# Routed attention, second pass: the row sums inverted on ScalarE by logarithm and exponential, VectorE's product one group later

## The chip, the cores and the metric

The kernel runs on one core of one Trainium2 chip. A time is microseconds (us) on the device from start to end of one execution of the whole program; the median of several runs counts. The engines named below are TensorE (PE; its weight loads are PEld), VectorE (DVE), ScalarE (ACT), GpSimd (POOL) and SyncE (SP), which issues most transfers.

## The reference, cut to what matters

A two-layer tower over 8 sequences of 512 rows with 192 features. The last layer's first half is the attention touched here: 12 heads of 16 features, softmax over 512 keys, then a projection and the residual add. Its second half sends each row to two of eight experts.

```python
x = x + _attention(_layer_norm(x, ln1_g, ln1_b), qkv_w, qkv_b, proj_w, proj_b)
    # attn = softmax(q @ k.T * 16 ** -0.5);  o = (attn @ v) merged over heads @ proj_w + proj_b
xn = _layer_norm(x, ln2_g, ln2_b).reshape(B * N, C)
    # top 2 of xn @ gate_w choose the experts of each row
return x + _moe_mlp(xn, gate_w, w1, b1, w2, b2).reshape(B, N, C)
```

The kernel doesn't divide the attention weights. It multiplies the exponentials with values that carry 16 columns of ones beside the 16 features of each head; so the read-out of a head has 16 rows of output and 16 rows that all hold the sum of the exponentials. The division comes after that, on 128 x 512 numbers for a group of four heads.

## The kernel before

The function `routed_attention` has two blocks. The first makes q, k and v and the row maxima of all batches; its last ScalarE instruction (L2272) is an exponential of one column, which brings in the table for the exponentials. The second block is the second pass, and the change is there. It is written out by hand, one program for each engine, unrolled over the eight batches (sequences) b. The engines are ordered among themselves by semaphores alone; a `Signal` counts in units per batch, and `x.wait(engine, b, k)` waits until k units of batch b are done. An engine works its own list strictly in order.

Heads come in three groups g of four (NG = 3), keys in four chunks c of 128 (T = 4). A tile n is one pair of group and chunk, n = 4 g + c, 0 to 11; it has two score tiles e = 2 n and e = 2 n + 1, each 128 keys x 2 heads x 512 queries.

- TensorE, for each n: the scores of tile n + 1 (L2500, four matmuls into PSUM; a score buffer is used again every third e, so scores e wait until exponential e - 3 is done); then the read-out of tile n (L2566), which needs the exponentials of n, summed over the four chunks of a group in one bank. Between these stands the rest of the previous batch: behind n = 2 and 3 the two halves of its projection (L2513), ahead of the second half the ranks of the batch before that (L2535, L2537), which wait for the first half's residual add; behind n = 8 and 9 the turning of its normed rows for the gate (L2519), the first of them waiting for the norm (`xa`) and for the copy of the present batch's group 1, whose bank it takes; behind n = 11 the gate's logits (L2527).
- ScalarE, for each e: the exponential (L2618, 128 x 1024). Behind e = 19 and 21 it copies the turned rows of the previous batch (L2611).
- VectorE, for each batch: sets up the residual rows, adds the previous batch's projection (L2646), with the ranks read between the halves and the places behind them, row statistics and norm constants (L2653 to L2658). Then for each group: ahead of g = 1 the norm (L2665), which waits for GpSimd's power (L2779); ahead of g = 2 the logits (L2678, L2682); then it waits for the group's read-out, copies it from PSUM to `OS` (L2730), makes a small read of it (L2732), shuffles the sums' rows over the outputs' rows into `OT` (L2734), takes their reciprocal (L2735) and multiplies it with `OS` in `OT` (L2736). The last product of a batch releases its projection (`ot`). Behind the groups it searches the two best logits of each row of the previous batch (L2688 to L2696).
- GpSimd: four indirect sends of rows, the power, four more sends, two products that scale the turned rows. The first sends of a batch wait for VectorE's places.
- SP loads the q and k of the batch after next when the scores of the present one are done.

Of the kernel before, what the change touches and what calls it, by code (L numbers as in the profile page):

```python
# [12 lines left out]
ALU = mybir.AluOpType  # L13
ACT = mybir.ActivationFunctionType
# [4 lines left out]
B, S, D = 8, 512, 192  # L19
# [5 lines left out]
NH, HD = 12, 16  # L25
NG, HG = 3, 4
# [1987 lines left out]
def routed_attention(nc, m, io):  # L2014
# [25 lines left out]
    spare = g2(P, [1])  # L2040
# [12 lines left out]
    sem = lambda name: SEMS.new(nc, name)  # L2053
# [3 lines left out]
    to, oq, pr, hh = Signal(nc, "qa_out_scaled", 1, 1), Signal(nc, "qa_out_rounded", 1, 1), \  # L2057
        Signal(nc, "qa_projected", 1, 2), Signal(nc, "qa_stream_updated", 1, 2)
    S1 = lambda n, per=1, credit=1: Signal(nc, f"ra_{n}", per, credit)
# [30 lines left out]
    def turned_parts(u, bank):  # L2090
        return (BT[:, 2 * u:2 * u + 2, :].rearrange("p b s -> p (b s)"), ps[0:3 * NH, bank, :].bitcast(BF16))
# [13 lines left out]
    with nc.Block(no_gpsimd_drain=True) as block:  # L2105
# [94 lines left out]
        @block.scalar  # L2200
        def _(act):
            for s in (xc, qc, vd, p1, to):
                s.start(act)
            for k in range(2):
                act.sem_inc(s_wr[k], 1)

            def scaled(b):
                oq.wait(act, b, 0)
                act.activation(TMP, OF[:, b, :, :], ACT.Identity, bias=magic, scale=inv3).then_inc(to.sem, 1)

            def deviation(some, n):

                act.wait_ge(s_v4, n)
                out = m.wk[2][:, some, :]
                if n % 2:
                    act.activation(out, m.var[:, some, :], ACT.Sqrt, bias=m.eps, scale=1.0 / D).then_inc(s_s4, 1)
                else:
                    act.activation(out, out, ACT.Sqrt, bias=m.eps).then_inc(s_s4, 1)

            def turned(b):  # L2220
                xt.wait(act, b, 1)
                for c in range(NC):
                    ins = act.activation(XT[b % 2][0:DC, c, :], ps[0:DC, banks(b, 0) + c, :], ACT.Identity,
                                         bias=gb[:, 1, c:c + 1], scale=gb[:, 0, c:c + 1])
                ins.then_inc(xc.sem, 1)

            for b in range(4):
                scaled(b)
            deviation(slice(0, 2), 1)
            scaled(4)  # L2230
            deviation(slice(0, 2), 2)
            scaled(5)
            act.wait_ge(s_w, 16 * (5 + HG))
            turned(0)
            scaled(6)
            for b in range(B):
                for k in range(2):
                    act.wait_ge(s_wr[k], 16 * 3 * b + 1)
                for s in range(2 * NC):
                    k, c = s // NC, s % NC  # L2240
                    if b == 0 and s == NC:
                        scaled(7)
                    if c == 0:
                        p2.wait(act, b, k - 1)
                    qp.wait(act, b, s + 1)
                    bank = ps[0:DC, banks(b, k) + c, :]
                    act.activation(QK[k][:, c, :], bank, ACT.Copy)
                    act.activation(PT[k][0][:, c, :], bank, ACT.Copy).then_inc(qc.sem, 1)
                for k in range(2):
                    rest.wait(act, b, k + 1)  # L2250
                    act.activation(PT[k][1], QK[k], ACT.Copy).then_inc(p1.sem, 1)
                if b + 1 < B:
                    turned(b + 1)
                if b == 0:
                    deviation(slice(2, B), 3)
                qp.wait(act, b, 5)
                Vb = V[:, b, :].rearrange("p (t h k d) -> p t h k d", t=T, h=NH, k=2)
                for u in range(2):
                    ins = act.activation(Vb[:, 2 * u:2 * u + 2, :, 0, :], ps[:, banks(b, 0) + u, 0:2 * D].rearrange(
                        "p (t h d) -> p t h d", t=2, h=NH), ACT.Copy)  # L2260
                act.activation(Vb[:, :, :, 1, :], m.one.to_broadcast([P, T * NH * HD]).rearrange(
                    "p (t h d) -> p t h d", t=T, h=NH), ACT.Copy)
                if b == 0:
                    deviation(slice(2, B), 4)
                    to.wait(act, B - 1, 1)
                ins = act.activation(ST_[b % 2][1][KR:KR + 3, 3 * (b // 2):3 * (b // 2) + 3, :], m.one[KR:KR + 3].to_broadcast(
                    [3, 3 * S]).rearrange("p (h s) -> p h s", h=3), ACT.Copy)
                ins.then_inc(vd.sem, 1)
            for u in range(AHEAD // 2):
                act.wait_ge(s_bt, u + 1)  # L2270
                act.activation(*turned_parts(u, 4 + u), ACT.Copy).then_inc(s_bc, 1)
            act.activation(spare, m.one, ACT.Exp)  # L2272

        @block.gpsimd
        def _(pool):
# [173 lines left out]
    OT, OS = g4(P, [NG, S]), g4(P, [NG, S])  # L2449
    VT = V.rearrange("p b (t h n) -> p b t h n", t=T, h=NH)  # L2450
    NS = NG * T
    st, ex, av = S1("scores_turned", 2 * NS, 2 * NS + 1), S1("exp", 2 * NS, 3), S1("read_out", NS, NS + 1)
    os_, sh, ot, pr, xx = S1("out_copied", NG), S1("sums_placed", NG), S1("out_normalised"), \
        S1("projected", 2), S1("x_stored", 2)
    s_l3 = sem("ra_out_chain")
    SG = lambda n, per=1: Signal(nc, f"ra_gate_{n}", per, 0)
    gv, gr, xa, gt, gc, lp, lc, mk, rk, po = SG("var"), SG("rstd"), SG("rows_normed"), SG("rows_turned", 2), \
        SG("rows_turned_copied", 2), SG("logits"), SG("logits_copied"), SG("masks"), SG("ranks"), SG("places")
# [10 lines left out]
    with nc.Block(no_gpsimd_drain=True) as block:  # L2469
# [135 lines left out]
        @block.scalar  # L2605
        def _(act):
            ex.start(act)
            def turned_copy(p, c, bank):
                gt.wait(act, p, c + 1)
                lp.wait(act, p, 0)  # L2610
                act.activation(XT2[:, c, :], ps[0:DC, bank, :], ACT.Identity, bias=gb2[:, 1, c:c + 1],  # L2611
                               scale=gb2[:, 0, c:c + 1]).then_inc(gc.sem, 1)

            for b in range(B):
                for e in range(2 * NS):
                    st.wait(act, b, e + 1)
                    av.wait(act, b, e // 2 - 1)
                    act.activation(PF[e // 2 % 2][:, 2 * (e % 2):2 * (e % 2) + 2, :],  # L2618
                                   ps[:, 2 * (e % 3):2 * (e % 3) + 2, :], ACT.Exp, scale=HD ** -0.5
                                   ).then_inc(ex.sem, 1)  # L2620
                    if b and e in (19, 21):
                        turned_copy(b - 1, e // 2 - 9, 7 - b % 2)
            turned_copy(B - 1, 0, 0)
            turned_copy(B - 1, 1, 2)
            act.wait_ge(s_sc[1], 16 * T * (B - 1))
            act.wait_ge(s_gb, 2 * B)
            act.activation(XA[B % 2][:, :, HEAD:RW], XA[1 - B % 2][:, :, HEAD:RW], ACT.Copy).then_inc(s_gb, 1)
            act.wait_ge(s_d, 1)
            act.activation(d, d, ACT.Exp).then_inc(s_e, 1)

        @block.vector
        def _(v):
# [4 lines left out]
            chain, gate = Link(v, s_l3), Link(v, s_gl)  # L2637
# [67 lines left out]
            def places(p):  # L2705
# [6 lines left out]
                    v.wait_ge(s_sc[1], 16 * T * (p - 1))  # L2712
                v.tensor_copy(POS[p % 2], IF).then_inc(po.sem, 1)

            for b in range(B):
                j, rows = b % 2, X[b % 2]
                for t in range(T):
                    chain(v.tensor_scalar(rows[:, t, :], m.H[:, b, t, :], m.mean[:, b, t:t + 1], m.rstd[:, b, t:t + 1],
                                          ALU.subtract, ALU.mult))
                chain(v.tensor_tensor(rows, rows, bp[:, None, :].to_broadcast([P, T, D]), ALU.add))  # L2720
                if b:
                    add_projection(b - 1)
                    constants(b - 1)
                for g in range(NG):
                    if b and g == 1:
                        norm(b - 1)
                    if b and g == 2:
                        logits(b - 1, 7 - j)
                    av.wait(v, b, T * (g + 1))
                    v.tensor_copy(OS[:, g, :], ps[:, 6 + (j + g) % 2, :]).then_inc(os_.sem, 1)  # L2730
                    os_.wait(v, b, g + 1)
                    v.tensor_scalar(spare, OS[:, g, 0:1], 1.0, None, ALU.mult)  # L2732

                    chain(v.stream_shuffle(OT[:, g, :], OS[:, g, :], mask=[HD + n % HD for n in range(32)]))  # L2734
                    chain(v.reciprocal(OT[:, g, :], OT[:, g, :]))  # L2735
                    ins = v.tensor_tensor(OT[:, g, :], OT[:, g, :], OS[:, g, :], ALU.mult)  # L2736
                ins.then_inc(ot.sem, 1)
                if b:
                    best_two(b - 1)

            read_ranks(B - 2, 5)
            places(B - 2)
# [337 lines left out]
```

## Time and profile before

| | |
|---|---|
| median of 3 runs | 2379.43 us (2377.87 to 2382.93) |
| profiled execution | span 2403.1 us from its first to its last instruction; the page gives no other time of it |
| busy share of the span | PE 78%, PEld 42%, VectorE 62%, ScalarE 45%, GpSimd 16% |
| second pass | from 1709 to about 2009 us of the span; exponentials from 1709.0 to 1971.3 us |
| in the pass | 192 exponentials, 185.1 us; 24 reciprocals, 80.5 us |

The page gives shares over the whole span, and its chain of waits covers only the last 30 us of the program, which lie in a later stage; what the pass is worth is seen from the pass alone: its groups of instructions, its busy time batch by batch, and the order of single instructions. Times in those views count from the span's start. A number in brackets behind an instruction is the time for which its engine stood idle before it, and what ended that.

### The profile page before, as it was taken

Reading aid. Unit: us, or ns where it says so; the run is one execution under the profiler, and the core shown is the slowest. Engines: PE = TensorE matmul, PEld = TensorE weight load, DVE = VectorE, ACT = ScalarE, POOL = GpSimd, SP = SyncE. Lnnn points to the kernel's source line nnn. Section 1 sums busy time; section 2 is a strip of 40 time slices with the busy share of each in tenths; the row PEclk is TensorE's granted clock in tenths of the full one; section 3 lists DMA queues with packets and bytes.
Section 4 is the critical chain, followed back from the end, with each engine's and each line's share of the span. In section 5 each row is a group of like instructions: output and inputs, shape, how many; then the busy total and the mean of one; then the engine's idle time right before and its main releaser. Section 6 shows DMA issues by size and latency. Waiting matters only on the chain. (4 is left out here: it accounts for less than half of the span.)

```text
span 2403.1 us, 30974 instructions
## 1 busy us (share of the span) xinstructions
PE 1879.3 (78%) x9780; PEld 1007.5 (42%) x9804; DVE 1495.5 (62%) x2518; ACT 1074.7 (45%) x1896; POOL 395.9 (16%) x595
## 2 busy tenths in 40 slices
PE   3868788858876453777668877998899984999994
PEld 2745655535333320000022234442133333888883
DVE  4558449966010687999878876999788883111114
ACT  1100222214110476999979964342477661222220
POOL 5000000000112010222100003331033343222221
PEclk8989999968887575555589978997799996999997
DMA  3011110005797004443011008777666703566664
GB/s 85 1 39 31 48 31 27 20 10 229 309 411 314 20 0 127 127 127 123 18 32 40 26 16 119 130 132 107 83 88 95 97 28 135 195 201 203 202 203 184
DMA packets 147792, 264.98 MB, mean 110 GB/s; under 512 B 28864, under 2 KB 115985, under 8 KB 142678
## 3 DMA queue, kind: packets, MB, share of 16 engines
q1 hardware_dynamic: 135750, 242.10, 38.0%
q0 software_dynamic: 10768, 18.19, 2.3%
q10 hardware_dynamic: 1152, 3.15, 0.3%
q8 instruction: 67, 1.10, 0.2%
q14 instruction: 55, 0.45, 0.1%
HBM read 221.85 MB, written 57.71 MB: 116 GB/s over the span
## 5 line engine op out<-in xcount | busy, mean ns | idle before, releaser
L1743 PE MATMUL ps<-arena 128*128 x376 | 194.9, 621 | 108.2 <-ACT ps L1785 60.1
L1785 ACT ACTIVATE ps<-ps,arena 128x512 f32<-128x512 f32 x384 | 256.7, 1121 | 6.3 <-POOL arena L1769 6.3
L1753 DVE TENSOR_REDUCE arena<-ps 128x1024 f32 x192 | 232.8, 1225 | 24.5 <-PE ps L1743 12.2
L1785 ACT ACTIVATION_READ_ACCUMULATOR ps<-ps,arena 128x1 f32 x384 | 234.7, 668 | 0.0
L2159 DVE TENSOR_REDUCE arena<-ps 128x1024 f32 x192 | 221.3, 1219 | 12.4 <-PE ps L2405 9.8
L2618 ACT ACTIVATE arena<-ps 128x1024 f32<-128x1024 f32 x192 | 185.1, 1020 | 97.6 <-PE ps L2500 96.4
L2962 DVE TENSOR_TENSOR arena<-ps,arena 128x384 f32<-128x384 f32 x39 | 21.8, 558 | 286.4 <-PE ps L2918 286.4
L2942 ACT ACTIVATE arena<-ps,arena 128x256 f32<-128x256 f32 x234 | 89.5, 481 | 235.9 <-PE ps L2907 230.0
L2405 PE MATMUL ps<-arena 96*128 96x512 bf16 x500 | 162.7, 430 | 26.4 <-DVE arena L2159 12.2
L1950 ACT ACTIVATE arena<-ps 128x1024 f32<-128x1024 f32 x192 | 178.7, 1048 | 7.8 <-DVE arena L1970 4.6
L529 PE MATMUL ps<-arena 96*128 96x456 f32 (+1 forms) x512 | 170.3, 482 | 8.8 <-DMA arena<-la_xt 5.2
L2918 PE MATMUL ps<-arena 128*128 128x192 f32 x936 | 162.5, 330 | 0.7 <-DVE arena L2962 0.7
L2918 PEld LDWEIGHTS ps<-arena 128*128 128x128 f32 x936 | 151.0, 190 | 13.6 <-issue 13.6
L1970 DVE TENSOR_SCALAR arena<-arena 128x1024 bf16<-128x1024 f32 x192 | 128.6, 691 | 28.9 <-ACT arena L1950 15.0
L1743 PEld LDWEIGHTS ps<-arena 128*128 128x128 bf16 x384 | 25.8, 111 | 276.8 <-ACT ps L1785 197.4
L529 PEld LDWEIGHTS ps<-arena 96*128 96x128 f32 x512 | 96.0, 196 | 71.8 <-issue 55.4
L1903 PE MATMUL ps<-arena 128*128 (+1 forms) x368 | 113.6, 389 | 15.7 <-DMA arena<-arena 13.3
L2877 POOL DMA_INDIRECT routed_out<-arena x78 | 74.8, 958 | 281.5 <-DVE arena L2962 269.6
L2903 PE MATMUL ps<-arena 128*128 128x256 f32 x468 | 110.0, 386 | 0.5 <-ACT arena L2942 0.5
L1225 DVE COPY arena<-ps 128x768 f32<-128x768 f32 x16 | 15.3, 958 | 152.1 <-PE ps L1276 152.1
L2566 PE MATMUL ps<-arena 128*32 128x512 f32 x768 | 105.2, 620 | 3.9 <-ACT arena L2618 2.1
L2500 PE MATMUL ps<-arena 99*128 99x512 bf16 x384 | 104.1, 395 | 2.4 <-ACTq L137 2.4
(394 smaller groups left out, 3264.8 us busy)
## 6 DMA issues: line engine op xcount, KB each, us to landing
arena<-in_sm_w_dram SPq DMA_DIRECT2D x128, 576.0 KB, 15.5
arena<-in_re_w_dram SPq DMA_DIRECT2D x39, 1252.0 KB, 5.9
arena<-ra_parts SPq DMA_DIRECT2D x192, 192.0 KB, 9.1
routed_in<-routed_in SPq DMA_DIRECT2D x8, 3332.0 KB, 14.2
ra_parts<-arena SPq DMA_DIRECT2D x48, 192.0 KB, 2.4
arena<-routed_in SPq DMA_DIRECT2D x39, 196.0 KB, 5.4
arena<-la_xt SPq DMA_DIRECT2D x16, 384.0 KB, 3.4
arena<-arena SPq DMA_DIRECT2D x64, 96.0 KB, 2.2
```

Source lines behind the costliest of these rows:

```text
L529: ins = pe.matmul(ps[:, 2 * (t % 2) + bank, to:to + w], XTs[j][:, c, t * P:(t + 1) * P], Wx[:, kind, c, at:at + w], start=(c == 0), stop=( ...
L1743: ins = pe.matmul(ps[:, 2 * (n % 4) + t % 2, :], QM[j][:, h, t * P:(t + 1) * P], KI[:, b, h // HG, :], start=True, stop=True)
L1753: v.tensor_reduce(MXq[:, b, 2 * u:2 * u + 2, at_head(h)], ps[:, 2 * (n % 4):2 * (n % 4) + 2, :], AX.X, ALU.max).then_inc(s_lk, 1)
L1785: ins = act.activation(bank, bank, ACT.Exp, bias=nb[n % 4][:, t % 2:t % 2 + 1], scale=c_reg, accum_out=RS[:, b, t, at_head(h):at_head(h) + 1])
L1903: ins = pe.matmul(ps[:, 2 * (n % 3) + q, :], QM[j][:, h, c * P:(c + 1) * P], QI[:, bass.ds(b, 1), g, :].rearrange("p o s -> p (o s)"), sta ...
L1950: act.activation(PF[n % 3], ps[:, 2 * (n % 3):2 * (n % 3) + 2, :].rearrange("p a s -> p (a s)"), ACT.Exp, scale=c_reg).then_inc(pe_.sem, 1)
L1970: v.tensor_scalar(PB[n % 3], PF[n % 3], MAGIC, MAGIC, ALU.add, ALU.subtract).then_inc(rd.sem, 1)
L2159: v.tensor_reduce(MX[:, bass.ds(b, 1), 2 * (n % 2):2 * (n % 2) + 2, n // 2].rearrange("p o t -> p (o t)"), ps[:, 2 * (n % 2):2 * (n % 2) + ...
L2405: ins = pe.matmul(ps[:, t, :], ST_[j][0][0:KR, h, t * P:(t + 1) * P], ST_[j][1][0:KR, h, :], start=True, stop=True)
L2618: act.activation(PF[e // 2 % 2][:, 2 * (e % 2):2 * (e % 2) + 2, :], ps[:, 2 * (e % 3):2 * (e % 3) + 2, :], ACT.Exp, scale=HD ** -0.5).then ...
L2903: pe.matmul(unit(k), wr[:, k * P:(k + 1) * P], XT[j][:, 0, :], start=True, stop=False)
L2918: ins = pe.matmul(ps[:, 7, h * D:(h + 1) * D], HT[j][:, k, h * P:(h + 1) * P], wr[:, at:at + D], start=(k == 0), stop=(k == KH - 1))
```

## The change

ScalarE inverts the row sums in place of VectorE. Of each group, VectorE still copies the read-out, and shuffles the sums into `OT`; the shuffle now signals `sh`. ScalarE waits for that, takes the natural logarithm of `OT` in place, waits for itself, and takes the exponential of the negative of it; that signals `iv`. VectorE's product waits for `iv`; it stands one group later: the product of group 0 behind the copy of group 1, that of group 1 behind the copy of group 2 and ahead of its shuffle, and that of group 2 behind the search for the two best. On ScalarE's list the inversion of group 0 stands ahead of e = 12, that of group 1 ahead of e = 20, and that of group 2 ahead of e = 2 of the next batch (for the last batch behind all exponentials). The one-column exponential in the first block becomes a load of the table set that has both functions.

```diff
-            act.activation(spare, m.one, ACT.Exp)
+            act.preload_act_table_set("natural_log_exp_and_others")
...
-    os_, sh, ot, pr, xx = S1("out_copied", NG), S1("sums_placed", NG), S1("out_normalised"), \
+    os_, sh, ot, pr, xx = S1("out_copied", NG), S1("sums_placed", NG, 0), S1("out_normalised"), \
         S1("projected", 2), S1("x_stored", 2)
-    s_l3 = sem("ra_out_chain")
+    s_l3, s_lg = sem("ra_out_chain"), sem("ra_sums_logarithm")
+    iv = S1("sums_inverted", NG, 0)
...
+            def invert(b, g):
+                sh.wait(act, b, g + 1)
+                act.activation(OT[:, g, :], OT[:, g, :], ACT.Ln).then_inc(s_lg, 1)
+                act.wait_ge(s_lg, NG * b + g + 1)
+                act.activation(OT[:, g, :], OT[:, g, :], ACT.Exp, scale=-1.0).then_inc(iv.sem, 1)
+
             for b in range(B):
                 for e in range(2 * NS):
+                    if b and e == 2:
+                        invert(b - 1, NG - 1)
+                    if e in (12, 20):
+                        invert(b, e // 8 - 1)
                     st.wait(act, b, e + 1)
...
+            invert(B - 1, NG - 1)
             turned_copy(B - 1, 0, 0)
...
+            def normalise(b, g):
+                iv.wait(v, b, g + 1)
+                ins = v.tensor_tensor(OT[:, g, :], OT[:, g, :], OS[:, g, :], ALU.mult)
+                if g == NG - 1:
+                    ins.then_inc(ot.sem, 1)
...
                     v.tensor_copy(OS[:, g, :], ps[:, 6 + (j + g) % 2, :]).then_inc(os_.sem, 1)
+                    if g:
+                        normalise(b, g - 1)
                     os_.wait(v, b, g + 1)
                     v.tensor_scalar(spare, OS[:, g, 0:1], 1.0, None, ALU.mult)
 
-                    chain(v.stream_shuffle(OT[:, g, :], OS[:, g, :], mask=[HD + n % HD for n in range(32)]))
-                    chain(v.reciprocal(OT[:, g, :], OT[:, g, :]))
-                    ins = v.tensor_tensor(OT[:, g, :], OT[:, g, :], OS[:, g, :], ALU.mult)
-                ins.then_inc(ot.sem, 1)
+                    v.stream_shuffle(OT[:, g, :], OS[:, g, :], mask=[HD + n % HD for n in range(32)]).then_inc(sh.sem, 1)
                 if b:
                     best_two(b - 1)
+                normalise(b, NG - 1)
```

## Rows read from the trace of the kernel before

**Rows 1.** Groups, 1709 to 1985 us: line, engine, shapes, count | busy us, mean ns | idle before.

```profile
L2618 ACT ACTIVATE arena<-ps 128x1024 f32<-128x1024 f32 x192 | 185.1, 1020 | 97.6 <-PE ps L2500 96.4
...
L2735 DVE RECIPROCAL arena<-arena 128x512 f32<-128x512 f32 x24 | 80.5, 3353 | 0.8
```

**Rows 2.** Busy time by stretch: length, PE, PEld, DVE, ACT, POOL, granted clock, DMA, GB/s.

```profile
1802.00:1836.00 34.00, 31.01 (x200) 12.40 (x200) 29.75 (x63) 24.45 (x26) 13.07 (x13) 1.00 0.72 98
...
1870.00:1906.00 36.00, 33.77 (x199) 12.65 (x199) 29.70 (x63) 24.45 (x26) 13.07 (x13) 0.91 0.65 88
```

**Rows 3.** Waits, 1709 to 1985 us: who, for whom, total us, times, longest.

```profile
PE ps L2519 <- DVE arena L2730: 10.8, 7, 1.8
```

**Rows 4.** Timeline of ScalarE: start, length, instruction, count, idle before and releaser.

```profile
1708.99 1.94 ACT L2618 ACTIVATE arena<-ps 128x1024 f32<-128x1024 f32 x2 [42.46 <-PE ps L2500]
...
1716.19 27.54 ACT L2618 ACTIVATE arena<-ps 128x1024 f32<-128x1024 f32 x28 [1.75 <-PE ps L2500]
...
1797.36 3.77 ACT L2618 ACTIVATE arena<-ps 128x1024 f32<-128x1024 f32 x4
1802.79 5.87 ACT L2618 ACTIVATE arena<-ps 128x1024 f32<-128x1024 f32 x6 [1.65 <-PE ps L2500]
...
1815.75 1.94 ACT L2618 ACTIVATE arena<-ps 128x1024 f32<-128x1024 f32 x2 [2.96 <-PE ps L2500]
1818.09 7.83 ACT L2618 ACTIVATE arena<-ps 128x1024 f32<-128x1024 f32 x8 [0.40 <-PE ps L2500]
```

**Rows 5.** Timeline of TensorE, 1800 to 1837 us.

```profile
1800.35 1.95 PE L2527 MATMUL ps<-arena 96*128 96x8 f32 x16
...
1808.16 2.22 PE L2513 MATMUL ps<-arena 128*128 128x192 f32 x12
...
1812.94 0.19 PE L2535 MATMUL ps<-arena 128*128 128x40 bf16 x1 [0.70 <-DVE arena L2646]
...
1815.12 1.03 PE L2500 MATMUL ps<-arena 99*128 99x512 bf16 x4
1816.45 1.06 PE L2566 MATMUL ps<-arena 128*32 128x512 f32 x8 [0.31 <-DVE arena L2646]
...
1827.00 0.61 PE L2519 MATMUL ps<-arena 128*96 128x128 f32 x4 [1.63 <-DVE arena L2730]
...
1834.25 1.95 PE L2527 MATMUL ps<-arena 96*128 96x8 f32 x16
```

**Rows 6.** Groups of ScalarE over the whole span, shapes kept apart.

```profile
L859 ACT ACTIVATE arena<-arena 128x528 f32<-128x528 f32 x32 | 20.6, 642 | 116.7 <-DVE arena L806 116.7
...
L2272 ACT ACT_TABLE_LOAD x1 | 1.3, 1283 | 0.0
```

**Rows 7.** Timeline of VectorE, 1800 to 1837 us.

```profile
1802.45 0.68 DVE L2730 COPY arena<-ps 128x512 f32<-128x512 f32 x1
...
1803.24 0.75 DVE L2734 STREAM_SHUFFLE arena<-arena 128x512 f32<-128x512 f32 x1
...
1807.41 0.69 DVE L2736 TENSOR_TENSOR arena<-arena 128x512 f32<-128x512 f32 x1
...
1809.57 0.19 DVE L2696 TENSOR_TENSOR arena<-arena 128x32 bf16<-128x32 f32 x1
...
1815.32 0.19 DVE L2702 TENSOR_TENSOR arena<-ps,arena 128x32 f32<-128x32 f32 x1 [2.43 <-PE ps L2513]
...
1820.11 0.73 DVE L2734 STREAM_SHUFFLE arena<-arena 128x512 f32<-128x512 f32 x1
```

**Rows 8.** Timeline of GpSimd, 1800 to 1837 us.

```profile
1822.64 1.05 POOL L2779 TENSOR_TENSOR arena<-arena 128x4 f32<-128x4 f32 x1
```

**Rows 9.** Timeline of all engines at the end of the exponentials, 1971 to 2015 us.

```profile
1979.37 0.69 DVE L2736 TENSOR_TENSOR arena<-arena 128x512 f32<-128x512 f32 x1
...
1980.20 4.18 PE L2513 MATMUL ps<-arena 128*128 128x192 f32 x12 [5.92 <-DVE arena L2736]
```

**Rows 10.** Busy time by stretch (columns as in rows 2), at the same place.

```profile
1975.00:1978.00 3.00, 0.00 (x0) 0.00 (x0) 2.93 (x5) 0.00 (x0) 0.00 (x0) 0.59 0.00 0
```

## The prediction

> **What bounds the kernel now.** I read the groups of the second pass first, then the busy time by batch, then one batch engine by engine. A batch has twelve tiles n, each with two score tiles e = 2n and 2n+1; ScalarE exponentiates the 24 score tiles one after the other, TensorE makes scores for n+1 and then reads out n. ScalarE's exponentials are 185.1 us of the pass and it stands idle 97.6 us before them, nearly all for TensorE's scores [rows 1]; 42.5 us of that lies ahead of the first [rows 4]. VectorE's reciprocals are the other large group, 24 of 3353 ns, 80.5 us [rows 1]. By batch, TensorE is busy 31.0 of 34.0 us, VectorE 29.8, ScalarE 24.5 [rows 2]. So TensorE sets the pace with ScalarE close behind it: eight exponentials in a row take 7.83 us, 0.98 each and 1.96 a tile [rows 4], and a tile's scores and read-out, 1.03 and 1.06 us on TensorE with some overlap, take about as long [rows 5]. With three score buffers TensorE can run ahead by one and a half tiles only; what delays an exponential by more than that reaches TensorE nearly in full.
>
> VectorE holds TensorE in few places: the turn of the routed rows waits for VectorE's copy, 10.8 us in seven batches, and in the batch shown TensorE stands 1.63 us there; the ranks wait 0.70 us for the residual add [rows 3, 5]. Elsewhere the reciprocals lie beside work that is later anyway. That is all that a faster VectorE can give back.
>
> **The change part by part.** I follow the batch of 1800 to 1834 on its old clock times, with TensorE at full clock as there [rows 2].
>
> *The inversion itself.* Ln and Exp over 128x512 f32 in the arena are not in the trace. Nearest row: 642 ns for 128x528 on ScalarE, arena to arena [rows 6]; as bounds, half an exponential of 1024 columns back to back, 0.49 [rows 4], and a whole one, 1.02 [rows 1]. I take 0.63, by the nearest. Between them Exp waits for Ln's signal: VectorE's chained reciprocals show idle time of 0.8 us in 24, 0.03 each [rows 1], ScalarE's wait on TensorE at 1818.09 shows 0.40 [rows 4]; I take 0.1. An inversion is 2 x 0.63 + 0.1 = 1.36 us, between 1.01 and 2.44; added work on an engine that already delays others can't give time back, so the low end is above nothing. There are 24, 32.6 us of ScalarE.
>
> *Third group, before e = 2 of the next batch.* ScalarE is free after e = 1 at 1797.36 + 3.77 = 1801.13 and idles 1.65 until 1802.79 [rows 4]. It now has to wait for the shuffle, which stands behind the logits (TensorE's product from 1800.35, 1.95 long), the copy of 1802.45 and, new in front of it, the product of group 1 (0.69, as at 1807.41, with 0.06 for its neighbours) [rows 5, 7]. The old shuffle ended at 1803.24 + 0.75 = 1803.99; the new one ends at 1804.7. The inversion then ends at 1806.1, and e = 2 starts 3.3 us late. TensorE has scores 4 done by 1804.6 but scores 5 need the buffer of e = 2, free at 1807.1: a pause of 2.6 us. From there tiles follow the exponentials: the first half of the projection starts at 1811.2 instead of 1808.16. Cost 3.0 us. The product that it needs (0.69 behind the inversion and the two-best search) is done by 1807.3, so the projection itself doesn't wait.
>
> *Between the halves of the projection.* The ranks' wait of 0.70 us was VectorE's backlog at the add; the search for the two best now ends 3.4 us sooner against the shuffle, so this goes: -0.7.
>
> *First group, before e = 12.* After the projection's second half VectorE has small work (ranks, add, places, statistics, constants), then copy and shuffle: from 1815.32 to 1820.11 + 0.73 = 1820.84, 5.5 us [rows 7]. None of this is shortened, for VectorE was idle 2.43 us ahead of it, waiting for TensorE [rows 7]. ScalarE has e = 11 done at 1815.75 + 1.94 = 1817.69 and used to go on at 1818.09 [rows 4]; now it waits until 1820.9 and inverts until 1822.25: e = 12 is 4.15 us late. TensorE gets through read-out 5 and scores 14 (1819.9), then stands until e = 12 is done at 1823.25, a pause of 3.35 us. Read-out 8 then ends near 1829.2, and the turn follows at once, because the norm that it waits for starts when GpSimd's power is done (1822.64 + 1.05) [rows 8] and the copy of group 1 ends at 1828.0. The turn began at 1827.00 before, its 1.63 us included: cost 2.25 us net. What is queued behind the waiting Ln is every exponential; what waits for those is TensorE.
>
> *Second group, before e = 20.* The shuffle is ready at 1829.7, before ScalarE has done e = 19 (1822.25 + 8 x 0.98 = 1830.1): no wait, only 1.36 us. It lies behind a copy that TensorE had to feed, and the turn gives ScalarE some slack; following e = 20 to 23, read-out 11 ends at 1837.7 and the logits start there, not 7.25 but 8.5 us after the turn [rows 5]: cost 1.25.
>
> *What goes or moves for nothing.* The reciprocals lay beside TensorE's work but for the waits just counted. The products keep their size and count; group 1's and 2's wait for inversions that are long done when VectorE gets there. The preload replaces a dummy exponential ahead of the pass, where ScalarE then idles 42.5 us [rows 4]; one table load of 1283 ns was there and one remains [rows 6]. GpSimd's sends hang on the places and SP's loads on the scores; both just come later with them. If the idle stretch ahead of the pass were gone, the load's 1.28 us would be paid, as it would have been before.
>
> *The sum.* A batch with a predecessor: 3.0 - 0.7 + 2.25 + 1.25 = 5.8; there are seven, 40.6 us (the first of them differs in detail, having no logits ahead of e = 2, and I give it the same). Batch 0 is bound by ScalarE, 28 exponentials without a gap [rows 4], and has two inversions: 2.7. At the end the projection waits 5.92 us, for the last product at 1979.37 [rows 9]: behind the last shuffle stood 3.4 for the reciprocal and 0.69; now 0.75 more stands ahead of that shuffle, and behind it the search for the two best (1808.10 to 1809.76 in rows 7, 1.7, longer than the inversion) and 0.69: -0.9. Together +42.4 us. The profiled execution has a span of 2403.1 us, 24 above the median of the runs, 2379.4, and the page gives no other time for it; a difference inside one pass I carry over unscaled: 2379.4 + 42.4 = 2421.8, say 2422. The bounds of an inversion move this by 24 x -0.35 = -8 and 24 x 1.08 = +26: 2414 to 2448 is the forecast's own range.
>
> **Rivals.**
>
> *The clock falls in the new pauses (20%).* In the loop of before, pauses of 1.63 us leave the granted clock at 1.00, 2.4 GHz, but in the stretch of the pause of 5.92 us at the end it is 0.59 on the mean, so mostly at 1.2 GHz, and the twelve matmuls after it take 4.18 instead of 2.22 us [rows 2, 5, 9, 10]. The new pauses of 2.6 and 3.35 us lie between. One batch of before with a spell at the low level took 36.0 instead of 34.0 us [rows 2], so a fall costs about 2.0. At one pause in each of seven batches that is 14 more, at both 28: 2436 to 2450, say 2443. The Trainium skill ("TensorE: Matmul & The Clock Gate", "Why this matters for your kernels") warns against just such idle gaps between bursts; by that rule this rival would be the likelier. The trace agrees for the long pause only.
>
> *The inversions vanish in ScalarE's idle time and VectorE's stalls go (6%): faster.* 97.6 - 42.5 = 55 us of ScalarE's idleness lie within the loop, against 32.6 of new work [rows 1, 4]. If every shuffle were there when ScalarE comes, and the inversion ran while TensorE projects or turns, only the gains would be left: 7 x (1.63 + 0.70) + 0.9 = 17 us, 2362. It decides at one place: the first shuffle would have to end by 1817.7 rather than 1820.84. Against it: ScalarE's idle stretches lie before e = 8, 10 and the turned copy, and only 0.40 us of idleness lies before e = 12 [rows 4].
>
> *The inversions cost their own time and no waits (6%).* 32.6 - 17 = +15: 2395. It needs the two long waits to be half of what I read.
>
> *Table loads around each inversion (4%): the change doesn't do what it says.* If Ln and Exp took two table sets, 24 x 2 loads of 1.28 us would come on top, 61.6 us, mostly on the path: 2483. Against it: the one load ahead of the pass serves all 192 exponentials and the turned copies among them, with no room between the eight in a row for another [rows 4, 6]. The Trainium skill's "ScalarE activation tables: per-element evaluation and per-set limits" ("Table sets in the compiler and the runtime") says that loads are placed per block by the longest run, with ties to the highest-index set, which need not keep to the preloaded set. No run here shows it; "ScalarE: Activation LUTs" ("Table sets: the hidden batching unit") lists one set with both functions, and by that this rival falls.
>
> **How the numbers follow.** Forecast 64%, clock 20%, faster 6%, own time only 6%, table loads 4%. The measurement can tell 0.2%, 4.8 us, from no change. Faster: 6% and 1% for sizes that I have all wrong, 0.07; within 0.2%: the low tail of "own time only", 0.03; slower 0.90. The range goes from 2394, the case without waits, to 2448, nearly all of the clock's case: left out are the faster case, the table loads and some 6% of the clock case above.
>
> **What would show it.** In the profile after: no RECIPROCAL of 3.35 us in the pass; 24 Ln and 24 Exp of 128x512 near 0.63 us, ScalarE's busy time in the pass up by 30; Ln waiting for VectorE's shuffle some 3 us before e = 12 and over 3 before e = 2, and nothing before e = 20; weight loads for the scores waiting longer for ScalarE; the batch near 39.7 us from logits to logits instead of 33.9 (1800.35 to 1834.25 in rows 5); the turn's wait for VectorE gone. I am wrong if the wait before e = 12 is under 1 us, if batches stay under 35 us, or if table loads stand in the pass. Granted clock under 0.95 in the batches would point to the first rival.

## The result, and the profile after

The changed kernel takes 2426.28 us (median of 4 runs, 2424.24 to 2434.7), the kernel before 2381.14 us beside it (4 runs): a ratio of 1.0201, 95% interval 1.0168 to 1.0233, or 45 us more. Forecast were 42.4 us more, 2422 us, range 2394 to 2448.

The two spans, 2403.1 and 2423.9 us, are only 20.8 us apart. The profiled execution of before lost time ahead of the pass, whose first exponential starts at 1709.0 us there and at 1684.3 in the changed kernel. Most of that was lost very early: the first instruction of a line between the embedding and the linear attention, in the views of that line before and after, starts at 129.6 and at 110.8 us.

```profile
L431 ACT ACTIVATE arena<-arena x2: 321/321/321, 129.6 to 532.7; 128x32 f32<-128x32 f32 x2
```

```profile
L431 ACT ACTIVATE arena<-arena x2: 321/322/322, 110.8 to 512.9; 128x32 f32<-128x32 f32 x2
```

So the pass is compared with itself: from its first exponential to the last small one behind it (the gate's, of 32 columns, at 2008.4 and 2029.1 us) it takes 299.4 us before and 344.8 after, 45.4 more, which is the difference of the medians (45.1).

The groups of the changed kernel in its pass (columns as in [rows 1]):

```profile
L2629 ACT ACTIVATE arena<-ps 128x1024 f32<-128x1024 f32 x192 | 182.7, 1022 | 90.2 <-PE ps L2501 90.1
...
L2619 ACT ACTIVATE arena<-arena 128x512 f32<-128x512 f32 x24 | 15.1, 629 | 0.8
L2617 ACT ACTIVATE arena<-arena 128x512 f32<-128x512 f32 x24 | 15.0, 626 | 48.1 <-DVE arena L2754 48.0
```

The reciprocals [rows 1] are gone; Ln (L2617) takes 626 ns and Exp (L2619) 629, with 0.8 us of idleness in 24 between them, 0.03 each: an inversion is 1.29 us. Ahead of Ln ScalarE stands 48.0 us for VectorE's shuffle. The waits' view counts them, and shows how long TensorE's weight loads for the scores wait for ScalarE, first before, then after:

```profile
PEld ps L2500 <- ACT arena L2618: 47.8, 56, 1.7
```

```profile
PEld ps L2501 <- ACT arena L2629: 88.2, 72, 3.6
ACT arena L2617 <- DVE arena L2754: 48.0, 15, 5.2
```

One batch of the changed kernel on ScalarE and on TensorE, to be held against [rows 4, 5]:

```profile
1835.10 0.63 ACT L2617 ACTIVATE arena<-arena 128x512 f32<-128x512 f32 x1 [3.35 <-DVE arena L2754]
1835.76 0.63 ACT L2619 ACTIVATE arena<-arena 128x512 f32<-128x512 f32 x1
1836.30 3.75 ACT L2629 ACTIVATE arena<-ps 128x1024 f32<-128x1024 f32 x4
...
1854.32 0.63 ACT L2617 ACTIVATE arena<-arena 128x512 f32<-128x512 f32 x1 [3.17 <-DVE arena L2754]
1854.98 0.63 ACT L2619 ACTIVATE arena<-arena 128x512 f32<-128x512 f32 x1
...
1865.36 0.62 ACT L2617 ACTIVATE arena<-arena 128x512 f32<-128x512 f32 x1
```

```profile
1830.97 1.95 PE L2528 MATMUL ps<-arena 96*128 96x8 f32 x16
...
1842.40 2.22 PE L2514 MATMUL ps<-arena 128*128 128x192 f32 x12
...
1846.41 0.19 PE L2536 MATMUL ps<-arena 128*128 128x40 bf16 x1
...
1856.58 0.61 PE L2501 MATMUL ps<-arena 99*128 99x512 bf16 x2 [3.10 <-ACT arena L2629]
1857.49 1.70 PE L2567 MATMUL ps<-arena 128*32 128x512 f32 x8 [0.31 <-ACT arena L2629]
1859.12 1.89 PE L2501 MATMUL ps<-arena 99*128 99x512 bf16 x4
...
1864.00 0.64 PE L2520 MATMUL ps<-arena 128*96 128x128 f32 x4
...
1871.99 1.95 PE L2528 MATMUL ps<-arena 96*128 96x8 f32 x16
```

ScalarE waits 3.35 us ahead of e = 2 and 3.17 ahead of e = 12, not at all ahead of e = 20. The ranks (L2536) and the turn (L2520) wait for VectorE no more, and the projection (L2514) doesn't wait for its product. Behind the pause of 3.10 us a read-out takes 1.70 us and a tile's scores 1.89, where [rows 5] has 1.06 and 1.03: TensorE is at its lower clock for a while. The busy time by stretch (columns as in [rows 2]) has 0.87 over the batch and 0.73 in these six microseconds:

```profile
1861.00:1902.00 41.00, 35.83 (x202) 12.37 (x205) 16.32 (x60) 27.57 (x33) 12.74 (x14) 0.87 0.57 79
...
1855.00:1861.00 6.00, 4.12 (x18) 0.77 (x22) 1.25 (x4) 5.08 (x6) 4.21 (x6) 0.73 0.15 50
```

A batch cut at TensorE's own marks (starts and ends in the timeline; us, means of the six intervals from one batch's logits to the next's in a profiled execution) shows where the time is. The last column is the pass, cut as above. It is one execution for each kernel, but it leaves out what lies ahead of the pass, which differs by up to 33 us between these executions. The kernels e1 to e9 follow below.

| kernel | logits to projection | projection, both halves | its end to the turn | turn to logits | batch | pass |
|---|---|---|---|---|---|---|
| before | 8.57 | 6.87 | 11.74 | 7.09 | 34.3 | 299.4 |
| after | 11.22 | 6.35 | 15.25 | 8.00 | 40.8 | 344.8 |
| e1 third group later | 9.13 | 6.35 | 15.54 | 7.99 | 39.0 | 332.2 |
| e2 first group later | 11.37 | 6.35 | 10.77 | 7.99 | 36.5 | 318.1 |
| e3 both later | 9.13 | 6.35 | 10.76 | 7.99 | 34.2 | 300.7 |
| e4 all late | 8.57 | 6.35 | 10.76 | 6.82 | 32.5 | 289.8 |
| e5 waits alone | 9.43 | 6.35 | 14.15 | 7.16 | 37.1 | 317.6 |
| e6 pauses filled | 11.46 | 6.35 | 13.67 | 7.99 | 39.5 | 339.5 |
| e7 no inversion | 8.22 | 6.35 | 10.48 | 6.80 | 31.9 | 282.6 |
| e8 product moved alone | 9.92 | 6.88 | 10.97 | 6.80 | 34.6 | 303.7 |
| e9 work alone | 7.69 | 6.35 | 10.49 | 7.96 | 32.5 | 291.5 |

### The profile page after: what moved, and what is told of

It is laid out like the page before. It is cut to its first block and busy times, and to the rows that moved or that the text cites. A ratio compares the mean times of both kernels' runs of the same rounds, so it can differ in the third digit from the quotient of the medians.

```text
span 2423.9 us, 30997 instructions
## 1 busy us (share of the span) xinstructions
PE 1897.0 (78%) x9780; PEld 1001.7 (41%) x9804; DVE 1392.8 (57%) x2494; ACT 1099.9 (45%) x1943; POOL 394.1 (16%) x595
## 5 line engine op out<-in xcount | busy, mean ns | idle before, releaser
L2501 PE MATMUL ps<-arena 99*128 99x512 bf16 x384 | 117.2, 420 | 32.2 <-ACT arena L2629 29.2
L2567 PE MATMUL ps<-arena 128*32 128x512 f32 x768 | 116.7, 683 | 10.3 <-ACT arena L2629 8.4
## 6 DMA issues: line engine op xcount, KB each, us to landing
routed_in<-routed_in SPq DMA_DIRECT2D x8, 3332.0 KB, 14.3
```

What stands on the lines that cost most here:

```text
L2501: ins = pe.matmul(ps[:, 2 * (e % 3) + q, :], ST_[j][1][0:KR + 3, h, c * P:(c + 1) * P], ST_[j][0][0:KR + 3, h, :], start=True, stop=True)
L2567: ins = pe.matmul(ps[32 * q:32 * q + 32, 6 + (j + g) % 2, :], VT[:, b, c_, h, :], PF[n % 2][:, q, :], start=(c == 0), stop=(c == T - 1))
```

## The experiments

Two theories stood against each other. Of the waits: the loss comes from ScalarE standing for a shuffle, with all exponentials queued behind it, ahead of e = 2 and e = 12. Of the work: 24 inversions on an engine close to the bound cost their time wherever they stand. Each time is given with its ratio to the kernel before on the same chip and the 95% interval.

**e1: the third group's inversion two exponentials later.**

```diff
-                    if b and e == 2:
+                    if b and e == 4:
                         invert(b - 1, NG - 1)
```

> The inversion of group 2 stands ahead of e = 4 of the next batch instead of e = 2. By then its shuffle should be done (it ends about 1.0 us before e = 3 does on the old times). Theory of the waits: the wait of 3.35 us goes, the stretch from the logits to the projection falls from 11.4 to about 9 us, seven times, so 17 to 20 us less than the changed kernel, about 2408 us. Theory of the work (it is ScalarE's 24 x 1.3 us that costs, wherever they stand): no change, 2426 us.

Measured 2419.33 us, 1.0146 (1.0105 to 1.0187). ScalarE doesn't wait there any more:

```profile
1834.78 1.94 ACT L2629 ACTIVATE arena<-ps 128x1024 f32<-128x1024 f32 x2 [1.70 <-PE ps L2501]
1836.61 0.63 ACT L2617 ACTIVATE arena<-arena 128x512 f32<-128x512 f32 x1
```

The first stretch falls by 2.1 us to 9.13, as the theory of the waits had it, but the batch only by 1.8, and the time, in ratio to the kernel before, by 13 us where 17 to 20 were expected. The inversion's own 1.29 us still stands in that stretch, and the stretch with the pause before e = 12 takes 0.3 more. The interval reaches up to that of the changed kernel, so here the trace decides and not the time.

**e2: the first group's inversion four exponentials later.**

```diff
-                    if e in (12, 20):
-                        invert(b, e // 8 - 1)
+                    if e in (16, 20):
+                        invert(b, e // 4 - 4)
```

> The inversion of group 0 stands ahead of e = 16 instead of e = 12; the others as in the changed kernel. Theory of the waits: its wait of 3.17 us before e = 12 goes, and TensorE's pause of 3.1 us with it; the stretch from the projection's end to the turn falls from 15.4 to 11.5 to 12 us, seven times: 24 to 27 us less than the changed kernel, about 2400 us. Theory of the work: no change, 2426 us.

Measured 2398.13 us, 1.0073 (1.0052 to 1.0095), 30 us of 48 gone in ratio to the kernel before (1.0201 to 1.0073). The stretch before the turn falls from 15.25 to 10.77, below the kernel before: in this stretch wait, low clock and the turn's old stall are all gone.

**e3: both moves.**

> Both moves, group 0 ahead of e = 16 and group 2 ahead of e = 4 of the next batch. Theory of the waits: both gains add, 41 to 47 us less than the changed kernel; 2380 to 2386 us, no more than 0.2% from the kernel before. Theory of the work: still 30 us above the kernel before, 2410 us or more. Granted clock in the batches back at 0.97 or more by the first, since the pauses are gone.

Measured 2384.04 us, 1.0019 (0.9999 to 1.0038): as expected by the waits, against the work's 2410. All 24 inversions are still there, of unchanged length, and of the 48.1 us of waiting ahead of them 5.2 are left:

```profile
L2617 ACT ACTIVATE arena<-arena 128x512 f32<-128x512 f32 x24 | 15.1, 628 | 5.2 <-DVE arena L2754 5.2
```

The granted clock over the exponentials of the pass is 0.96 where 0.97 or more was expected: it still falls behind the logits in some batches.

**e4: every inversion where its shuffle is done and ScalarE has slack.**

```diff
-                    if b and e == 2:
-                        invert(b - 1, NG - 1)
-                    if e in (12, 20):
-                        invert(b, e // 8 - 1)
+                    if b and e in (2, 4):
+                        invert(b - 1, e // 2)
+                    if e == 16:
+                        invert(b, 0)
...
+            invert(B - 1, 1)
             invert(B - 1, NG - 1)
```

> Group 0 ahead of e = 16, group 1 ahead of e = 2 of the next batch (where ScalarE idles 1.65 us for TensorE's logits), group 2 ahead of e = 4 of the next batch. Theory of the waits: as with both moves, and the inversion of group 1 costs nothing, another 0.5 to 0.9 us a batch: 2375 to 2381 us, level with the kernel before or up to 0.3% faster. Theory of the work: 2410 us or more.

Measured 2373.41 us, 0.9968 (0.995 to 0.9986): faster than both kernels, 0.3% against the one before. The inversion of group 1 now runs where ScalarE used to idle for the logits; 0.51 us of that idleness is left:

```profile
1814.26 0.66 ACT L2617 ACTIVATE arena<-arena 128x512 f32<-128x512 f32 x1
1814.95 0.63 ACT L2619 ACTIVATE arena<-arena 128x512 f32<-128x512 f32 x1
1816.09 1.94 ACT L2629 ACTIVATE arena<-ps 128x1024 f32<-128x1024 f32 x2 [0.51 <-PE ps L2501]
1817.91 0.63 ACT L2617 ACTIVATE arena<-arena 128x512 f32<-128x512 f32 x1
```

**e5: the waits without the work.** Ln and Exp take 16 of 512 columns; the other sums stay uninverted.

```diff
-                act.activation(OT[:, g, :], OT[:, g, :], ACT.Ln).then_inc(s_lg, 1)
+                act.activation(OT[:, g, 0:16], OT[:, g, 0:16], ACT.Ln).then_inc(s_lg, 1)
                 act.wait_ge(s_lg, NG * b + g + 1)
-                act.activation(OT[:, g, :], OT[:, g, :], ACT.Exp, scale=-1.0).then_inc(iv.sem, 1)
+                act.activation(OT[:, g, 0:16], OT[:, g, 0:16], ACT.Exp, scale=-1.0).then_inc(iv.sem, 1)
```

> The changed kernel with Ln and Exp of an inversion on 16 of the 512 columns, at the same places and with the same waits (the other columns stay the sums, uninverted). What is left of the loss is the waits. An ACTIVATE of so few columns is about 0.2 us, so an inversion falls from 1.28 to about 0.45 us. Theory of the waits: the two waits before e = 2 and e = 12 stay above 3 us, and about two thirds of the loss stay, 28 to 32 us above the kernel before: 2409 to 2413 us. Theory of the work: two thirds of the loss go, 15 us above, 2396 us.

Measured 2401.93 us, 1.0099 (1.0063 to 1.0134), between the two expectations and in neither. The waits are as long as with the full work:

```profile
1807.05 0.21 ACT L2617 ACTIVATE arena<-arena 128x16 f32<-128x16 f32 x1 [3.17 <-DVE arena L2754]
...
1827.19 0.22 ACT L2617 ACTIVATE arena<-arena 128x16 f32<-128x16 f32 x1 [3.35 <-DVE arena L2754]
```

So half of the loss goes with the work although the waits stay. The batch is 3.7 us shorter than in the changed kernel. Some 2.5 of that is the shorter inversion, 0.8 at each of its three places: behind a wait, nothing hides the work. The rest is TensorE's clock, which falls behind the logits in no batch of this trace. Behind the pause before e = 12, here 2.27 us long, it fell in five of the six batches, and that stretch took 14.3 to 14.5 us in them; in the sixth it stayed at 1.00, and the stretch took 12.85. The same six microseconds, counted from 0.64 us ahead of the pause's end, in a batch with the fall and in the one without:

```profile
1882.60:1888.60 6.00, 5.07 (x22) 0.88 (x22) 1.25 (x4) 5.25 (x6) 4.27 (x6) 0.72 0.15 50
1920.00:1926.00 6.00, 5.06 (x34) 1.20 (x34) 2.60 (x9) 6.00 (x7) 4.33 (x6) 1.00 0.16 53
```

**e6: TensorE kept busy in the two pauses.** The scores are made five times over at e = 4 and seven times at e = 14, with the same result.

```diff
-                for q in range(2):
+                for q in [0, 1] * {4: 5, 14: 7}.get(e, 1):
```

> The changed kernel with TensorE's scores made five times over at e = 4 and seven times at e = 14, that is in the two pauses that the waits make (1.7 and 2.6 us of matmuls more, same results). If the falls of the granted clock behind the pauses cost time, as the first rival had it, the clock stays at 1.00 there and 7 to 10 us come back: 2416 to 2419 us. If the falls lie beside waits anyway, no change, 2426 us, or a few us more from the added matmuls.

Measured 2420.03 us, 1.0174 (1.0121 to 1.0226); the interval holds the changed kernel's 1.0201, so the time alone doesn't decide. The trace does for the pause before e = 12. TensorE, then the granted clock in the six microseconds that had 0.73 above:

```profile
1812.78 3.19 PE L2501 MATMUL ps<-arena 99*128 99x512 bf16 x14
1816.49 0.60 PE L2501 MATMUL ps<-arena 99*128 99x512 bf16 x2 [0.51 <-ACT arena L2629]
1817.40 1.07 PE L2567 MATMUL ps<-arena 128*32 128x512 f32 x8 [0.31 <-ACT arena L2629]
```

```profile
1815.00:1821.00 6.00, 5.18 (x30) 1.29 (x29) 1.74 (x5) 6.00 (x7) 4.23 (x6) 1.00 0.15 52
```

The clock stays at 2.4 GHz, the stretch falls from 15.25 to 13.67 us, 1.6 a batch, the same difference that e5 shows between its own batches. The stretch behind the logits gains nothing (11.46). In the two traces the clock falls there in most batches, beginning around the logits' 16 small matmuls and before the pause, so that filling the pause doesn't prevent it; the kernel before has such falls too, without any pause [rows 2]. The fall costs time here as well: in the one batch of e6 without it the stretch takes 10.26 us, in the others 11.05 to 12.67.

**e7: no inversion at all.** The product takes the sums as they are, behind the shuffle; neither reciprocal nor Ln and Exp.

```diff
             def normalise(b, g):
-                iv.wait(v, b, g + 1)
+                sh.wait(v, b, g + 1)
```

(The three calls of the inversion are left out as well.)

> The changed kernel without any inversion (the product takes the sums as they are and waits for the shuffle alone): neither reciprocal nor Ln and Exp. It shows the most that a freed VectorE could give. Theory of the waits: only the turn's 1.63 us and the ranks' 0.70 us a batch and 1 to 3 us at the end come back, 13 to 19 us under the kernel before: 2362 to 2368 us. If VectorE were a bound of its own in the pass, as its 88% of busy time could suggest, much more: 40 us or more under it.

Measured 2363.89 us, 0.9951 (0.9928 to 0.9974): 15 us under the kernel before in the medians, within the waits' 13 to 19. Freeing VectorE of 80 us, with the product moved, is worth no more than this (21 us against e8 below, which moves the product and keeps the reciprocals); VectorE's high busy share was not a bound of its own.

**e8: the product moved, the reciprocal kept on VectorE.**

```diff
-                    v.stream_shuffle(OT[:, g, :], OS[:, g, :], mask=[HD + n % HD for n in range(32)]).then_inc(sh.sem, 1)
+                    chain(v.stream_shuffle(OT[:, g, :], OS[:, g, :], mask=[HD + n % HD for n in range(32)]))
+                    chain(v.reciprocal(OT[:, g, :], OT[:, g, :]))
```

(The inversions and their waits are left out.)

> The second part of the change alone: VectorE keeps its reciprocal behind each shuffle, ScalarE inverts nothing, and only the products stand one group later, as in the changed kernel. Theory of the waits: nothing waits for a shuffle on ScalarE, so batches stay within 1 us of the kernel before; the turn's wait shrinks by the 0.7 us of a product, the projection's first half comes up to 1.7 us later because its last product stands behind the search for the two best; 2375 to 2390 us. If the moved product were a cause of the loss, 2400 us or more.

Measured 2385.32 us, 1.0039 (1.0018 to 1.0059), as expected. The projection comes 1.35 us later, since TensorE now stands some 2.2 us ahead of it for the product, and the stretch before the turn is 0.77 shorter: the moved product is a small cost by itself, 9 us in ratio. In the changed kernel the projection doesn't wait for it, so it is no cause of the loss there.

**e9: the work without the waits.** The kernel of e7 with Ln and Exp of 128x512 back at the changed kernel's places, on a scratch tile of ones (23 of them: the one behind all exponentials is left out).

```diff
-                sh.wait(act, b, g + 1)
-                act.activation(OT[:, g, :], OT[:, g, :], ACT.Ln).then_inc(s_lg, 1)
+                act.wait_ge(iv.sem, NG * b + g + 1)
+                act.activation(SCR, SCR, ACT.Ln).then_inc(s_lg, 1)
                 act.wait_ge(s_lg, NG * b + g + 1)
-                act.activation(OT[:, g, :], OT[:, g, :], ACT.Exp, scale=-1.0).then_inc(iv.sem, 1)
+                act.activation(SCR, SCR, ACT.Exp, scale=-1.0).then_inc(iv.sem, 1)
```

> The kernel without inversion, with ScalarE's Ln and Exp put back at the changed kernel's places (ahead of e = 2, 12 and 20) but on a scratch tile of ones that nothing else uses: the work of 24 inversions without a wait for a shuffle. To be read against the kernel without inversion, 2364 us. Theory of the waits: ahead of e = 2 it fits into ScalarE's 1.65 us of idleness, ahead of e = 12 and 20 it costs up to 1.3 us each, and batch 0 pays 2.6: 12 to 20 us more, 2376 to 2384 us, far from 2426. Theory of the work: all 31 us of it and more, 2395 us or above.

Measured 2376.71 us, 1.0002 (0.998 to 1.0025): level with the kernel before. ScalarE takes the inversions ahead of e = 12 and of e = 2 without idling (the first and the second Ln here):

```profile
1799.10 0.63 ACT L2617 ACTIVATE arena<-arena 128x512 f32<-128x512 f32 x1
...
1815.84 0.65 ACT L2617 ACTIVATE arena<-arena 128x512 f32<-128x512 f32 x1
...
1817.64 5.87 ACT L2630 ACTIVATE arena<-ps 128x1024 f32<-128x1024 f32 x6 [0.49 <-PE ps L2501]
```

Against e7, ahead of e = 2 it costs nothing (7.69, and 7.69 is what e7 has in four batches of six), ahead of e = 12 nothing (10.49 for 10.48), ahead of e = 20 1.16 us (7.96 for 6.80).

**The account.** In ratios to the kernel before, times 2380 us: freeing VectorE -12 us (e7, 0.9951). The work alone +12 on top (e9, 1.0002). The waits with next to no work +35 on top of e7 (e5, 1.0099). Both together are +59 over e7 (1.0201), 12 more than the two apart. Each ratio has an interval of 0.002 to 0.004 on either side, so the parts are good to some 10 us, and the 12, which come from four ratios, aren't clear of zero by the times alone. The passes give the same picture: -16.8 (e7 to before), +8.9, +35.0 and +62.2, 18 more than the two apart. The stretches say where these come from: behind a wait the work ahead of e = 2 and e = 12 is paid for (0.8 us at each place between e5 and the changed kernel) where e9 pays nothing, and the clock falls more often than in e5. What lies behind the pass takes 394 to 397 us in all eleven traces, so the uninverted sums of e5, e7 and e9 didn't change the time of the later stages.

## Why the prediction was right

**The mechanism** was read right, wait by wait: 3.35 us ahead of e = 2, 3.17 ahead of e = 12 ("over 3" and "some 3"), none ahead of e = 20, and no table load in the pass. The inversion was put at 1.36 us and is 1.29. The rivals without waits and with table loads are out by the trace of the changed kernel, the theory of the work by e3, e4 and e9. Not read right were TensorE's clock and, with it, one of the two pauses: that before e = 12 was put at 3.35 us and is 3.10; that behind the logits was put at 2.6, and is 2.02 in one of the six batches and 0.4 to 0.9 in five, because TensorE has slowed down ahead of it.

**Logits to projection**, 3.0 forecast: 3.4 against the batch that was followed (7.81 in [rows 5]), 2.65 in the mean, since the kernel before has slow batches too. In one batch of the changed kernel (logits at 1750.04) the clock is back before ScalarE's wait is over, and the stretch takes 10.25 us, as in e6's batch without a fall; in the five others it takes 11.4. So the mechanics at full clock cost 2.4, 0.6 less than forecast, and the falls about 1.1 in five of six batches.

**Between the halves**, -0.7: measured -0.5 in the mean; the ranks' wait is gone.

**End of the projection to the turn**, 2.25: measured 3.5. This is the term that was mis-sized, and e5 and e6 say why. With TensorE kept at 2.4 GHz the stretch is 13.67, 1.93 over the kernel before, so the forecast's mechanics were 0.3 too high; the low clock behind the pause adds 1.6. The first rival's mechanism is therefore true for this pause, at 1.6 instead of 2.0 us, some 11 us in seven batches. That a fall of the clock was left a rival and not put into the sum was the error here. The prediction's own sign for that rival, a granted clock under 0.95 in the batches, came true (0.87). For the other pause the rival is right that the clock falls and costs time, but not that the pause is what brings the fall: it begins before the pause in most batches, as it does without a pause in the slow batch of before from which the 2.0 us were read.

**Turn to logits**, 1.25: measured 0.9.

**The rest.** The six intervals together grew from 205.6 to 244.9 us, 39.3, where 6 x 5.8 = 34.8 was forecast. Batches 0, 1 and the end of the exponentials grew by 8.0 (8.5). What follows the last exponential came down from 38.1 to 36.2 us, -1.9 (-0.9); the last product released the projection after 4.50 us of waiting instead of 5.92 [rows 9]. The sum is 45.4. That the forecast came within 3 us is therefore in part luck: the clock's cost, which it left out, stood against terms that were put too high and against falls that the kernel before has too.

## What to carry to other kernels

Work that is moved to an engine with idle time costs little if it stands where its operand is ready, and much if the engine has to wait for it with its own queue behind: the same 24 inversions cost +2.0% at one set of places and gained 0.3% at another, two to six exponentials later (all against the kernel with VectorE's reciprocals). Find in the trace when the producer's instruction ends and when the consumer gets there, and move the consumer behind the later of the two. An engine that is 88% busy can still be off the path; taking 80 us from it gave 12 to 15, with the product moved in the same step.

## What the runs showed of the hardware

After a pause of 3.10 us TensorE's granted clock falls, but not at one fixed place. In the batch of the changed kernel above, the scores directly behind the pause still run at full speed (0.61 us for two matmuls), the read-out and the scores after them take 1.70 and 1.89 us, and 5.5 us behind the pause's end a tile's scores are at 1.04 again. In e1 the same pause is in some batches followed by slow matmuls at once, 1.03 us for the two:

```profile
1855.77 1.03 PE L2501 MATMUL ps<-arena 99*128 99x512 bf16 x2 [3.10 <-ACT arena L2629]
```

Shorter pauses have no fixed outcome either: behind 2.27 us the clock fell in five of six batches (e5), at the one of 2.17 us ahead of e8's projection in two of six, and a pause of 1.63 us in the kernel before leaves it at 1.00 [rows 2, 5]. It also falls behind the logits' 16 small matmuls without a pause, in most batches of the changed kernel.

Ln on 128x512 costs the same as Exp, 626 and 629 ns, a fifth of VectorE's reciprocal of the same tile (3353 ns, [rows 1]) each, and two of them with a semaphore between have a gap of 0.03 us.
